# Graph network on one core: four consecutive edges summed on one partition before the scatter product

## The reference, cut to what matters

```python
edge_messages = jax.nn.relu(edge_input @ W1.T + b1)              # layer 0; edge_input = [x[dst], x[src], edge_attr, u]
aggregated = jax.ops.segment_sum(edge_messages, dst, num_segments=x.shape[0])
...
h = jax.nn.relu(m_in @ msg_w1 + msg_b1)                          # layer 1; m_in = [x[row], x[col], edge_attr]
summed = jax.ops.segment_sum(h @ msg_w2 + msg_b2, col, num_segments=num_nodes)
counts = jax.ops.segment_sum(jnp.ones(...), col, num_segments=num_nodes)
```

## Time and profile before

| | |
|---|---|
| median of three runs | 3970.87 us (3970.52 to 3974.17) |
| profiled execution | 3971.81 us, its span 3970.1 us |
| mean granted TensorE clock | 0.558 |
| busy: TensorE, VectorE, ScalarE, GpSimd | 3202.5, 1601.3, 587.7, 2967.9 us |
| gathers | 3126, 2954.4 us busy |

### The profile page before, as it was taken

How to read it: one execution, slowest core, us unless ns; L and a number is a source line. 1 busy time by engine, 2 the same in 40 slices (tenths; PEclk the granted TensorE clock), 3 DMA queues, 4 the chain that set the end, 5 groups by cost and what they waited for, 6 DMA issues and landing times.

```text
span 3970.1 us, 47116 instructions
## 1 busy us (share of the span) xinstructions
PE 3202.5 (81%) x16880; PEld 2994.1 (75%) x16880; DVE 1601.3 (40%) x3988; ACT 587.7 (15%) x1005; POOL 2967.9 (75%) x3156
## 2 busy tenths in 40 slices
PE   6888888878888787887877888888888888878877
PEld 6778777777787777776767777777777777777776
DVE  6444444444444444444433334343433333333333
ACT  2111111111111111111111111111111111111111
POOL 6777777777777777777767777777777777777776
PEclk7555555565555666566655555555555555565556
DMA  8544444444444444445444444444444444444443
GB/s 287 151 139 139 138 138 146 138 141 142 146 138 145 145 145 141 146 141 154 123 139 139 138 139 138 138 142 138 139 126 150 133 144 142 136 140 141 141 141 97
DMA packets 290895, 567.96 MB, mean 143 GB/s; under 512 B 166678, under 2 KB 186625, under 8 KB 265692
## 3 DMA queue, kind: packets, MB, share of 16 engines
q1 hardware_dynamic: 173928, 344.29, 26.3%
q0 software_dynamic: 100032, 205.00, 19.9%
q10 hardware_dynamic: 16692, 15.57, 1.1%
HBM read 545.14 MB, written 19.45 MB: 142 GB/s over the span
## 4 chain that ended last, share of the span: by engine, by line
POOL 71%; issue 23%; DMA 3%; PE 1%; DVE 1%; ACT 0%; SPq 0%; DVEq 0%; POOLq 0%; ACTq 0%
POOL Qr L251 71%; DMA Qr<-tabQ,srcE 2%; DMA srcE<-in_srcL 0%; DVE BIG L1131 0%; PE bank L922 0%; DMA tabP<-BIG 0%; PE bank L909 0%; DMA BIG<-tabP 0%; PE bank L196 0%; DMA BIG<-in_dstR 0%; DVE bank L227 0%; DVE BIG L231 0%; PE bank L199 0%; PE bank L867 0%; PE bank L914 0%
## 5 line engine op out<-in xcount | busy, mean ns | idle before, releaser
L251 POOL DMA_INDIRECT Qr<-tabQ,srcE x3126 | 2954.4, 945 | 982.2 <-issue 946.7
L909 PE MATMUL bank<-wall,BIG 128*128 128x128 f32 x6256 | 1482.3, 412 | 22.4 <-DMA BIG<-tabP 22.4
L1131 DVE TENSOR_TENSOR BIG<-bank,Qr 128x512 f32<-128x512 f32 x782 | 540.1, 691 | 2299.2 <-DMA Qr<-tabQ,srcE 2279.5
L922 PE MATMUL bank<-BIG 128*128 128x42 f32 x6256 | 1387.9, 398 | 66.7 <-ACT BIG L1036 64.8
L922 PEld LDWEIGHTS bank<-BIG 128*128 128x128 f32 x6256 | 1320.0, 311 | 117.0 <-ACT BIG L1036 108.2
L909 PEld LDWEIGHTS bank<-wall,BIG 128*128 128x128 f32 x6256 | 1318.9, 310 | 26.6 <-issue 26.6
L914 PE MATMUL bank<-BIG 126*128 126x128 bf16 x3128 | 505.6, 296 | 648.0 <-DVE AC L1149 647.0
L1036 ACT ACTIVATE BIG<-BIG 128x512 f32<-128x512 f32 x782 | 492.5, 630 | 3275.7 <-DVE BIG L1131 3274.3
L914 PEld LDWEIGHTS bank<-BIG 126*128 126x128 bf16 x3128 | 376.2, 139 | 749.0 <-DVE AC L1149 705.0
L1051 DVE TENSOR_TENSOR BIG<-bank,BIG 126x512 bf16<-126x512 f32 x782 | 533.8, 683 | 18.0 <-DMA BIG<-in_dstR 18.0
L1122 DVE TENSOR_TENSOR BIG<-bank,relE 128x168 f32<-128x168 f32 x782 | 252.3, 323 | 0.0
(11 more groups left out here) (112 smaller groups left out, 520.3 us busy)
## 6 DMA issues: line engine op xcount, KB each, us to landing
BIG<-in_eaT SPq DMA_DIRECT2D x194, 1024.0 KB, 5.6
BIG<-in_dstR SPq DMA_DIRECT2D x194, 504.0 KB
Qr<-tabQ,srcE POOLq DMA_INDIRECT x3126
BIG<-tabP SPq DMA_DIRECT2D x782, 31.5 KB
tabP<-BIG SPq DMA_DIRECT2D x12, 384.0 KB, 3.5
tabQ<-BIG ACTq DMA_DIRECT2D x17, 256.0 KB, 4.5
tabP<-BIG ACTq DMA_DIRECT2D x11, 384.0 KB, 2.8
X<-in_xN SPq DMA_DIRECT2D x1, 3136.0 KB, 13.8
```

The lines of the kernel that those rows point to most:

```text
L251: e.indirect_dma_start(Q[0:p, i % R_Q, j, :], None, tabQ[l][:, :], bass.IndirectOffsetOnAxis(ap=srcE[0:p, g, j:j + 1], axis=0)).then_inc(f ...
L909: e.matmul(bank[i % R_C][:, j * D:(j + 1) * D], f_eaT[:, k % R_EA, (g % LQ * J + j) * P:(g % LQ * J + j + 1) * P], wc[l], start=(j == 0), ...
L922: last = e.matmul(bank[4 + i % 2][:, 0:W], M[:, i % R_M, j, :], S[:, i % R_S, j, :], start=(j == 0), stop=(j == J - 1))
L1131: e.tensor_tensor(M[:, i % R_M, :, :].rearrange("p j d -> p (j d)"), bank[i % R_C][:, :], Q[:, i % R_Q, :, :].rearrange("p j d -> p (j d)" ...
```

## The change: what it does

The edges are laid out differently: partition p of a group holds the four consecutive edges 4p to 4p + 3 rather than edges p, 128 + p, 256 + p, 384 + p. Since edges are sorted by destination, the four have mostly one destination; the new form allows at most two (the one of the first edge and the one of the last), and `checks` tests that. Let m0..m3 be the four messages, and k0..k2 1 where the edge's destination differs from that of the last edge, else 0 (m4 holds them, and a quarter of their count in its last column). VectorE makes t = (m0 + m2) + (m1 + m3) and b = k0 m0 + k1 m1 + k2 m2. With S1 the one-hot of the last edge, S0 that of the first and SD = S0 - S1, the group's sum is t x S1 + b x SD: two f32 scatter products for four. The count is 4 x (SD x (k0 + k1 + k2)/4 + S1), one bf16 product as before, with SC made on VectorE in place of the reduce. `runs` holds the five steps.

In the loop VectorE's order becomes: ST, S, the five steps for g - 2, SD, accumulate g - 4, SC, add Q to g - 1. The scatter moves to iteration g - 3 and all due times by one. M has two buffers for three; TB (t and b) has three. TensorE now waits for the PSUM bank explicitly and for the tabP rows only before the second tile. The last group's valid edges lie on 80 partitions of four tiles, where they filled 128, 128 and 64 of three tiles.

```diff
@@ gathers
-                for j in range(tiles(g)):
-                    p = VP if g == NG - 1 and j == VJ else P
+                p = VP if g == NG - 1 else P
+                for j in range(J):
                     e.indirect_dma_start(Q[0:p, i % R_Q, j, :], None, tabQ[l][:, :],
...
@@ checks (ahead of the loop)
+                    e.tensor_tensor(m4, relE[:, :, :], relE[:, :, J - 1:J].broadcast_to([P, NGP, J]), ALU.not_equal)
...
+                    link(e.tensor_tensor(ne, relE[:, :, 1:J - 1], relE[:, :, 0:1].broadcast_to([P, NGP, J - 2]), ALU.not_equal))
...
+                    link(e.tensor_tensor(ne, ne, m4[:, :, 1:J - 1], ALU.mult))
+                    e.tensor_reduce(stat[:, 5:6], ne.rearrange("p g j -> p (g j)"), AX, ALU.max)
...
+                    link(e.tensor_reduce(m4[:, :, J - 1], m4[:, :, 0:J - 1], AX, ALU.add))
+                    link(e.tensor_scalar(m4[:, :, J - 1], m4[:, :, J - 1], 1.0 / J, None, ALU.mult))
@@ TensorE
-                        for j in range(J):
-                            last = e.matmul(bank[4 + i % 2][:, 0:W], M[:, i % R_M, j, :], S[:, i % R_S, j, :], start=(j == 0), stop=(j == J - 1))
+                        e.wait_ge(v_tb, STEPS * (i + 1))
+                        o = bank[4 + i % 2]
+                        e.matmul(o[:, 0:W], TB[:, i % R_T, 0, :], S[:, i % R_S, 1, :], start=True, stop=False)
+                        last = e.matmul(o[:, 0:W], TB[:, i % R_T, 1, :], SD[:, i % R_S, :], start=False, stop=True)
                         if l == 0:
-                            last = e.matmul(bank[4 + i % 2][:, W:2 * W], onesb[:, :], S16[:, i % R_S, :], start=True, stop=True)
+                            last = e.matmul(o[:, W:2 * W], foursb[:, :], SC[:, i % R_S, :], start=True, stop=True)
@@ VectorE
+            def runs(e, i, l, g):
+                m, t, b, k = M[:, i % R_M, :, :], TB[:, i % R_T, 0, :], TB[:, i % R_T, 1, :], STEPS * i
+                e.wait_ge(v_rl, i + 1)
+                e.tensor_tensor(b, m[:, 2, :], m4[:, g, 2:3].broadcast_to([P, D]), ALU.mult).then_inc(v_tb, 1)
+                e.tensor_tensor(M2, m[:, 0:2, :], m[:, 2:4, :], ALU.add).then_inc(v_tb, 1)
+                e.wait_ge(v_tb, k + 1)
+                e.scalar_tensor_tensor(out=b, in0=m[:, 1, :], scalar=m4[:, g, 1:2], in1=b, op0=ALU.mult, op1=ALU.add).then_inc(v_tb, 1)
+                e.wait_ge(v_tb, k + 2)
+                e.tensor_tensor(t, M2[:, 0, :], M2[:, 1, :], ALU.add).then_inc(v_tb, 1)
+                e.wait_ge(v_tb, k + 3)
+                e.scalar_tensor_tensor(out=b, in0=m[:, 0, :], scalar=m4[:, g, 0:1], in1=b, op0=ALU.mult, op1=ALU.add).then_inc(v_tb, 1)
...
-                        rel = relE[:, g, :].unsqueeze(2).broadcast_to([P, J, W])
-                        io = bank[6][:, NGP:NGP + W].unsqueeze(1).broadcast_to([P, J, W])
-                        e.tensor_tensor(S[:, i % R_S, :, :], io, rel, ALU.is_equal).then_inc(v_s, 1)
+                        ends = relE[:, g, 0:J:J - 1].unsqueeze(2).broadcast_to([P, 2, W])
+                        io = bank[6][:, NGP:NGP + W].unsqueeze(1).broadcast_to([P, 2, W])
+                        e.tensor_tensor(S[:, i % R_S, :, :], io, ends, ALU.is_equal).then_inc(v_s, 1)
+                    if 2 <= g < NG + 2:
+                        runs(e, l * NG + g - 2, l, g - 2)
...
+                        e.tensor_tensor(SD[:, i % R_S, :], S[:, i % R_S, 0, :], S[:, i % R_S, 1, :], ALU.subtract).then_inc(v_sd, 1)
...
-                                e.tensor_reduce(S16[:, i % R_S, :], S[:, i % R_S, :, :].rearrange("p j w -> p w j"), AX, ALU.add).then_inc(v_cn, 1)
+                        e.scalar_tensor_tensor(out=SC[:, i % R_S, :], in0=SD[:, i % R_S, :], scalar=m4[:, g, J - 1:J],
+                                               in1=S[:, i % R_S, 1, :], op0=ALU.mult, op1=ALU.add).then_inc(v_sc, 1)
```

More of the change, by code:

```diff
@@ L33 @@
 NA = NT + P
-VOID = NP + 7
+VOID = NP + P - 1
 EPS = 1e-5
@@ L37 @@
 NC = len(CH)
-R_EA, R_PB, R_BC, R_Q, R_ST, R_S, R_M, R_PT, R_U = 2, 4, 2, 10, 3, 6, 3, 4, 2
-R_C = 3
+R_EA, R_PB, R_BC, R_Q, R_ST, R_S, R_M, R_PT, R_U = 2, 4, 2, 10, 3, 6, 2, 4, 2
+R_C, R_T = 3, 3
 PF = R_Q
@@ L43 @@
 VALID = E - (NG - 1) * GE
-VJ, VP = VALID // P, VALID % P
+VP = VALID // J
 UN = [(b, 4) for b in range(0, 44, 4)] + [(44, 2), (46, NB - 46)]
@@ L48 @@
 READY = [min(NG, math.ceil(NG * math.sqrt(min(N, (b + n) * P) / N)) + 2) for b, n in UN[:-1]] + [NG]
-DUE = [g + 3 for g in READY]
+DUE = [g + 4 for g in READY]
 def due(i, lag):
@@ L80, in build @@
         onesb = sb("onesb", [P, P], BF16)
+        foursb = sb("foursb", [P, P], BF16)
         zero = sb("zero", [P, 192])
@@ L101, in build @@
         flagI = sb("flagI", [1, 1], I32)
-        stat = sb("stat", [P, 5])
-        vio = sb("vio", [P, 5])
+        stat = sb("stat", [P, 6])
+        vio = sb("vio", [P, 6])
         vsum = sb("vsum", [P, 1])
         BIG = sb("BIG", [P, NBIG])
+        m4 = dstE[:, :, :].rearrange("p g j -> p (g j)").bitcast(F32).rearrange("p (g j) -> p g j", j=J)
         def w(name):
@@ L141, in edge_sems @@
         def edge_sems(l):
-            return {n: sem(f"{n}{l}") for n in ("C", "st", "s", "cn", "tt", "rl", "A", "ag")}
+            return {n: sem(f"{n}{l}") for n in ("C", "st", "s", "sd", "sc", "tb", "tt", "rl", "A", "ag")}
         fs = edge_sems(0)
@@ L236, in pieces_sync @@
                 e.dma_start(node_rows(tabP[l], c), P3[:, c % R_PT, 0:n, :]).then_inc(s_tabP[l][c % R_PT], 16)
-        def tiles(g):
-            return -(-VALID // P) if g == NG - 1 else J
         def q_count(i):
-            return 16 * sum(tiles(x % NG) for x in range(i % R_Q, i + 1, R_Q))
+            return 16 * J * (i // R_Q + 1)
         def gathers(e, l, g0, g1):
@@ L341, in checks @@
                 flat = relE[:, :, :].rearrange("p g j -> p (g j)")
-                full = (NG - 1) * J + VJ
+                full = (NG - 1) * J
+                ne = sq[:, 0:NGP * (J - 2)].bitcast(F32).rearrange("p (g j) -> p g j", j=J - 2)
                 if i == 2:
@@ L762, in build @@
         M, at = carve(at, [R_M, J, D])
-        S, at = carve(at, [R_S, J, W])
-        S16, at = carve(at, [R_S, W], BF16)
+        S, at = carve(at, [R_S, 2, W])
+        SD, at = carve(at, [R_S, W])
+        SC, at = carve(at, [R_S, W], BF16)
+        TB, at = carve(at, [R_T, 2, D])
+        M2, at = carve(at, [2, D])
         ST, at = carve(at, [R_ST, GE], BF16)
@@ L779, in build @@
         fPT = fO
-        v_C, v_st, v_s, v_cn, v_tt, v_rl, v_A, v_ag = (fs[n] for n in ("C", "st", "s", "cn", "tt", "rl", "A", "ag"))
+        v_C, v_st, v_s, v_sd, v_sc, v_tb, v_tt, v_rl, v_A, v_ag = (
+            fs[n] for n in ("C", "st", "s", "sd", "sc", "tb", "tt", "rl", "A", "ag"))
+        STEPS = J + 1
         u_y, u_f, u_v, u_var, u_sd, u_nm, u_n, u_t, u_tc, u_q, u_qv, u_o = (
@@ L1117, in fast_vector @@
                             rows_hot(e, i + 1)
-                        if g > 3:
-                            e.wait_ge(v_ag, i - 3)
-                        rel = relE[:, g, :].unsqueeze(2).broadcast_to([P, J, W])
-                        io = bank[6][:, NGP:NGP + W].unsqueeze(1).broadcast_to([P, J, W])
-                        e.tensor_tensor(S[:, i % R_S, :, :], io, rel, ALU.is_equal).then_inc(v_s, 1)
[L1123 to L1127, removed]
-                                e.tensor_reduce(S16[:, i % R_S, :], S[:, i % R_S, :, :].rearrange("p j w -> p w j"), AX, ALU.add).then_inc(v_cn, 1)
[L1129 to L1132, removed]
+                        if g > 4:
+                            e.wait_ge(v_ag, i - 4)
+                        ends = relE[:, g, 0:J:J - 1].unsqueeze(2).broadcast_to([P, 2, W])
[3 more added lines that the diff above has]
+                        runs(e, l * NG + g - 2, l, g - 2)
+                    if g < NG:
+                        i = l * NG + g
+                        e.wait_ge(v_s, i + 1)
+                        e.tensor_tensor(SD[:, i % R_S, :], S[:, i % R_S, 0, :], S[:, i % R_S, 1, :], ALU.subtract).then_inc(v_sd, 1)
                     if l == 1 and g % 16 == 15 and g // 16 < NC:
@@ L1138, in fast_vector @@
                         last_terms(e, g // 16)
[L1139 to L1142, removed]
+                    if 4 <= g < NG + 4:
+                        i = l * NG + g - 4
+                        if (g - 4) % LQ == 0:
+                            at = bases(mybir.EngineType.DVE, g - 4)
                         e.wait_ge(v_A, i + 1)
-                        if i and (g <= 3 or g >= NG):
+                        if i and (g <= 4 or g >= NG):
                             e.wait_ge(v_ag, i)
@@ L1147, in fast_vector @@
                             e.wait_ge(s_mz, NU)
-                        acc = AC[:, 0:ctl, bass.ds(at[(g - 3) % LQ], W)]
+                        acc = AC[:, 0:ctl, bass.ds(at[(g - 4) % LQ], W)]
                         e.tensor_tensor(acc, acc, bank[4 + i % 2][:, 0:ctl * W].rearrange("p (t w) -> p t w", w=W),
                                         ALU.add).then_inc(v_ag, 1)
```

(11 more changed lines are left out.)

39 lines of the change are left out of this document (22 added, 17 removed).

## The result

The changed kernel takes 4034.22 us (median of four runs, 4032.7 to 4035.9) against 3971.4 for the kernel before (now also four runs, 3970.52 to 3974.17): ratio 1.0157, interval [1.0139, 1.0175], 63 us slower. Forecast were 4015 and a range of 3975 to 4110.

What follows compares the result with a forecast made beforehand. GpSimd's back-to-back gathers, one each 1.25 us, were taken as the bound. 3971.8 us plus 40 for held gathers in the loop plus 4.5 for the ends gave 4016.3, against the median 4015; range 3975 to 4110.

Steps and rivals of the forecast that it cites:

- The bound, and what is removed: Line 251's gathers on GpSimd set the pace; dropping two of four TensorE scatter products, 735 us, is worth 0.
- VectorE has room: VectorE's added steps in each group finish 2.95 us after the addition of Q began, leaving 2 of 4.99 us spare.
- What reaches the gathers: VectorE steps with two SBUF inputs, running across a gather's start, lengthen that gather, and the chain loses that time.
- the form e - 0.12: A gather lengthens by the VectorE instruction's end after the gather's start, less 0.12 us, if that instruction began first.
- The size: Gathers held by new VectorE steps in the loop: 0.051 us a group, 40 us; 9 to 51 by required head start.
- the third rival: The five VectorE steps hold a gather as one: 0.49 us a group, 380 us, total 4355; chance 0.06.
- the groups in step: Groups without delayed landing: the next group's last gather, 2.40 us after the addition, meets the last step, costing 0.06 us.
- Ends: Outside the steady loop: checks 0, two more gathers 2.5 us, steps replacing products 0.2 per layer end; together 4.5 us.
- The first (no stretch): Rival: VectorE steps fall between gather starts, so gathers are not lengthened; not slower, 3975 us; chance 0.11.
- the second: Rival: a VectorE step holds a gather for its whole duration; 0.225 us a group, 176 us, total 4151; chance 0.07.

Runs made afterwards that it cites:

- the twins: Kernel before plus five unused VectorE additions a group: with both inputs in SBUF 4070.32 us, with one input in PSUM 3971.99 us.

## Why the prediction was right, point by point

- *The bound, and what is removed.* Right. Line 251's idle time did not move; TensorE at 65% (forecast 63) gave back nothing. It lost 574 us of busy time. The prediction has 735 in one place and 694 in another, without a working for the second.
- *VectorE has room.* Right: 1378.5 us of waiting are left, 1.76 us a group. Durations were off: a step with a scalar operand from SBUF took 347 ns and the first step 293, not 281, so that in the median group the last step began 2.40 us behind the addition of Q, not 2.30.
- *What reaches the gathers.* Right, and shown by the twins: two inputs in SBUF 97 us, one in PSUM nothing. Where the gather came free with the instruction it began under, the form e - 0.12 (e the end of that instruction after the gather's start) holds to 0.02 us in all but two of 291 gathers. How long before the gather an instruction had to begin was another matter: 0.01 us for line 1079, 0.03 for 1075, 0.04 for 1074, and 0.06 to 0.08 for the two with a scalar operand, where 0.04 had been taken for all.
- *The size.* The term of 40 us for the loop was mis-sized: stretches grew by 60.0 - 3.9 = 56.1 us. The step that failed is the sum's assumption that a gather comes free with the instruction it began under. Taken so, the held gathers give 41.1 us, 1.6 of it in the node update, which is the forecast's 40; the other 18.9 us come from gathers passed over by the instructions behind. This is the third rival, "the five steps hold as one", in 108 of 400 held gathers, mostly over one instruction; it had been priced as all or nothing at 380 us. That the 40 were met has some luck in it. The steps were longer than reckoned, and had to begin longer before a gather, which work against each other. And for the groups in step the prediction had the next group's last gather meet the last step 0.10 after its start and lose 0.06 each time. The measured mean, over the 386 groups whose addition began under 1.8 us behind the last gather, is 0.059, but it is made otherwise: in the median group the last step began just as that gather did (medians 2.40 and 2.39 us behind the addition). 330 of the 386 were not held, or came free with the instruction they began under, and lost 4.4 us in all; the 56 that were passed over lost 18.4.
- *Ends.* 4.5 us forecast. The checks cost 1.6 on the gathers, as worked out; the first addition (74.59 for 73.10) made none wait long. Two gathers 2.5. The turn took 1.6 and the tail 1.2 more, where 0.2 each had been put down. These had been counted as steps against products, without the iteration by which the due times moved; that this iteration is the reason was not tested. About 7 us.
- *The rule of the Trainium skill* (SBUF — State Buffer, "Who interferes with whom"): which instructions contend is confirmed by the twins. Its whole duration, which would have given 4151, is not what the traces show where a gather comes free with its own instruction: it is then held 0.12 us less than to that instruction's end. With instructions in a row the stretch can pass the whole duration (0.83 us under an instruction of 0.27).
- *The rivals.* The first (no stretch) fell by the trace; the second by the form. With what was measured in place of the two terms the sum is 4015 + 16.1 (56.1 for 40) + 2.4 (6.9 for 4.5), 4033 or 4034; measured 4034.

## What to carry to other kernels

Where GpSimd's indirect DMAs set the pace, look at each gather longer than its neighbours and at the VectorE instruction running at its start before adding VectorE work, even if VectorE is half idle. Instructions with both tensors in SBUF are the ones to count; with one of them in PSUM the same work cost nothing here, and where that can't be had, a short gap between two of them lets the gather in: with gaps the changed kernel still lost 39 us, but not 63. Taking work from an engine that is busiest but not on the chain is worth nothing until the chain's own cadence is shortened.

## What the runs showed of the hardware that was not expected

- A gather that waits need not get in when the instruction it waits for ends: 91 of 94 from under line 1081 came free only with the 42-element instruction behind it, yet 52 of 54 from under line 1077, with the same kind of operands and another instruction 0.26 us behind it, came free at once. A wait that is already met makes no difference (66 of 70), an idle gap does (none passed over in four traces). With the addition of Q behind line 1081, one of its inputs in PSUM, all came free at once (79 and 85). What tells the two places apart is open.
- In one session a chip ran the kernel before in 4834 us, and in a later one in 3978. Whoever compares kernels here needs the kernel before in the same session.
